# A ring of 20 batches in a kernel's second part, and a load moved between the value transfers of its first

## The reference

```python
x = x + xattn(_layernorm(x), ctx_1024, Wq, Wk, Wv, Wo)
x = x + ffn(_layernorm(x), weight, bias)

def ffn(x, weight, bias):
    w_scale = jnp.mean(jnp.abs(weight))
    q_weight = jnp.sign(weight) * (jnp.abs(weight) > 0.5 * w_scale)
    i_scale = jnp.max(jnp.abs(x)) / 127.0
    q_input = jnp.clip(jnp.round(x / i_scale), -128.0, 127.0)
    return jnp.einsum('bsk,ok->bso', q_input, q_weight) * w_scale * i_scale + bias
```

## Time and profile before

| | us |
|---|---|
| median of 3 runs | 1137.72 |
| profiled execution | 1138.31 |
| its span, first to last instruction | 1136.5 |
| PE busy | 1075.1 (95%) |
| DVE busy | 1015.8 (89%) |
| ACT busy | 963.0 (85%) |
| POOL busy | 729.6 (64%) |
| DMA queue of SP, share of 16 engines | 68.2% |
| moved | 262.97 MB |

### The profile page before, as it was taken

How to read it: one execution, slowest core, us unless ns; L and a number is a source line. 1 busy time by engine, 2 the same in 40 slices (tenths; PEclk the granted TensorE clock), 3 DMA queues, 4 the chain that set the end, 5 groups by cost and what they waited for, 6 DMA issues and landing times.

```text
span 1136.5 us, 44893 instructions
## 1 busy us (share of the span) xinstructions
PE 1075.1 (95%) x14007; PEld 865.5 (76%) x14007; DVE 1015.8 (89%) x1836; ACT 963.0 (85%) x2147; POOL 729.6 (64%) x1547
## 2 busy tenths in 40 slices
PE   7998999999999999999999999999599999999991
PEld 6997988988989988998889998998455555555540
DVE  4653898999999999999999999999789999999981
ACT  4564888988989889988899989999599999999980
POOL 4675998999999999999999999999500000000000
PEclk9999999999999999999999999999599999999996
DMA  8765366666676666766667653432049999999996
GB/s 290 228 176 162 85 205 189 211 189 214 177 223 183 210 216 187 221 194 198 207 195 222 184 154 106 121 104 67 1 180 408 421 424 426 426 407 371 411 395 267
DMA packets 119897, 262.97 MB, mean 231 GB/s; under 512 B 65193, under 2 KB 76649, under 8 KB 99378
## 3 DMA queue, kind: packets, MB, share of 16 engines
q1 hardware_dynamic: 119810, 262.44, 68.2%
q10 hardware_dynamic: 48, 0.07, 0.0%
HBM read 139.79 MB, written 122.64 MB: 231 GB/s over the span
## 4 chain that ended last, share of the span: by engine, by line
POOL 34%; issue 24%; PE 12%; ACT 9%; DMA 8%; DVE 6%; SPq 3%; POOLq 1%; ACTq 1%; DVEq 0%
POOL qa_sb L559 6%; POOL pw_sb L589 6%; POOL qr_sb L599 5%; ACT x_sb L789 5%; PE y_ps L1113 5%; DMA out_y<-x_sb 5%; POOL pw_sb L605 4%; POOL os_sb L619 3%; POOL o_sb L610 3%; DVE x_sb L1052 3%; ACT x_sb L772 2%; DMA x_sb<-out_y 2%; POOL ve_sb L576 2%; SPq L378 2%; POOL rs_sb L583 2%
## 5 line engine op out<-in xcount | busy, mean ns | idle before, releaser
L1258 PEld LDWEIGHTS xT_ps<-wqs,xT_sb 128*128 128x128 f32 x2048 | 239.2, 192 | 48.3 <-ACT xT_sb L725 48.3
L1258 PE MATMUL xT_ps<-wqs,xT_sb 128*128 128x128 f32 x2048 | 263.6, 282 | 2.8 <-ACT xT_sb L725 2.8
L978 DVE SCALAR_TENSOR_TENSOR x_sb<-x_sb,mv_sb,y_ps 128x512 f32 (+1 forms) x256 | 177.9, 736 | 3.2 <-PE y_ps L1250 3.2
L789 ACT ACTIVATE x_sb<-x_sb,mean 128x512 f32 (+1 forms) x256 | 168.7, 707 | 0.0
L1273 PE MATMUL pT_ps<-v_blk,pT_sb 128*128 128x102 f32 (+1 forms) x1280 | 163.6, 275 | 0.0
L689 ACT ACTIVATE sq_sb<-x_sb 128x512 bf16 (+1 forms) x256 | 160.8, 628 | 1.0 <-DVE x_sb L978 0.8
L1273 PEld LDWEIGHTS pT_ps<-v_blk,pT_sb 128*128 128x128 f32 x1280 | 155.2, 194 | 1.7 <-ACT pT_sb L738 1.0
L985 DVE TENSOR_REDUCE amax<-x_sb (+1 forms) x128 | 155.1, 1213 | 0.0
L748 ACT ACTIVATE e_sb<-e_sb,rs_sb 128x308 f32<-128x308 f32 x256 | 127.3, 544 | 16.2 <-DVE e_sb L961 6.6
L725 ACT ACTIVATE xT_sb<-xT_ps 128x1024 f32<-128x1024 f32 x128 | 131.3, 1026 | 3.0 <-PE xT_ps L1180 2.9
L1317 PE MATMUL sc_ps<-wT,x_sb 64*128 64x512 f16 x1024 | 133.5, 380 | 0.1
(11 more groups left out here) (140 smaller groups left out, 2286.0 us busy)
## 6 DMA issues: line engine op xcount, KB each, us to landing
out_y<-x_sb SPq DMA_DIRECT2D x112, 1024.0 KB, 10.2
x_sb<-in_x SPq DMA_DIRECT2D x128, 512.0 KB, 5.1
x_sb<-out_y SPq DMA_DIRECT2D x48, 1024.0 KB, 15.3
x_sb<-in_ctx SPq DMA_DIRECT2D x38, 256.0 KB, 4.5
k_blk<-k_scr SPq DMA_DIRECT2D x256, 9.6 KB, 1.7
v_blk<-v_scr SPq DMA_DIRECT2D x256, 10.2 KB
v_scr<-x_sb SPq DMA_DIRECT2D x38, 68.0 KB, 3.1
k_scr<-x_sb SPq DMA_DIRECT2D x38, 64.0 KB, 3.4
```

Source lines behind the costliest of these rows:

```text
L789: act.activation(u_sb[:, k % 2, t, :], x1_sb[:, bass.ds(x1_turn(g, k) + t * E, E)], ACT.Identity, bias=stat_of(mean1, j, t, back)).then_in ...
L978: dve.scalar_tensor_tensor(out=x1_at(kj, gj, t), in0=x_sb[:, kj // 2, 2 * (kj % 2) + t, :], scalar=mv_sb[:, kj, t, 0:1], in1=y_ps[:, t, :] ...
L1258: last = pe.matmul(bank[0][:, t * HD:(t + 1) * HD], xT_sb[:, t, c, :], wqs[:, c, :], start=c == 0, stop=c == EC - 1)
```

## The change

The ring x1_sb gets 20 slots, of which the last four are x_sb: x1_sb grows by four batches and x_sb becomes its tail, so the sum is the same. The temporaries of the second part move to the place of the first part's working tiles (from xT_sb on; four tables are moved so that the allocation covers them). In the first part x1_sb still turns over its first 16 slots (KEPT_TURNS = 4). In the second part, RING is 5, and four of the stored batches are read into x's slots as soon as `added_t` says that x is no longer needed there; the other 44 are read twenty batches behind a slot's result, not sixteen.

In the first part the first half of the next batch's x is issued between the eighth and the ninth of the twelve value pieces. A cycle of SP was: both halves of x(b), store, 12 values of b-1, 4 keys of b. It becomes: second half of x(b), store, 8 values of b-1, first half of x(b+1), 4 values of b-1, 4 keys of b.

```diff
-SLOTS = 16
-KEPT = SLOTS
+KEPT = 16
+KEPT_TURNS = KEPT // XS
+SLOTS = KEPT + XS
 RING = SLOTS // XS
...
-        x_sb = sb("x_sb", [P, XS, TPB, E])
...
         x1_sb = sb("x1_sb", [P, SLOTS * TPB * E])
+        x_sb = x1_sb[:, KEPT * TPB * E:].rearrange("p (k t e) -> p k t e", k=XS, t=TPB)
+
+        with nc.sbuf_tensor("qm_sb", [P, 2, 2, E], F32) as qm_sb, \
+                nc.sbuf_tensor("q16T_sb", [P, 2 * TPB, EC, P], F16) as q16T_sb, \
+                nc.sbuf_tensor("u_sb", [P, 2, TPB, E], F32) as u_sb, \
+                nc.sbuf_tensor("st_a", [P, NT], F32) as st_sb:
+            pass
...
         def x1_turn(g, k):

-            return ((g + (B - KEPT) // XS) % RING) * (XS * TPB * E) + k * TPB * E
+            return (g % RING) * (XS * TPB * E) + k * TPB * E
...
+            def x_half(b, k, n):
+
+                at_least(sp, added_t, 4 * (b - XS) + 2 * n + 2)
+                sp.dma_start(x_sb[:, k, 2 * n:2 * n + 2, :].rearrange("p t e -> p (t e)"),
+                             xv[bass.ds(b, 1), :, 2 * n:2 * n + 2, :].rearrange("b p t e -> p (b t e)"))\
+                  .then_inc(x_in[2 * k + n], 16)
+
             def batch_step(b, k, g, store=True):

-                for n in range(2):
-                    at_least(sp, added_t, 4 * (b - XS) + 2 * n + 2)
-                    sp.dma_start(x_sb[:, k, 2 * n:2 * n + 2, :].rearrange("p t e -> p (t e)"),
-                                 xv[bass.ds(b, 1), :, 2 * n:2 * n + 2, :].rearrange("b p t e -> p (b t e)"))\
-                      .then_inc(x_in[2 * k + n], 16)
+                x_half(b, k, 1)
                 if store:
                     store_x1(b - XS, k, g - 1)
+                v_fetch(b - 1, k - 1, SEGS[:8])
+                if not isinstance(b, int) or b + 1 < B:
+                    x_half(b + 1, (k + 1) % XS, 0)
+                v_step(b - 1, k - 1, SEGS[8:])
+                k_fetch(b, k)
...
+            x_half(XS, 0, 0)
             with sp.Fori(1, (B - KEPT) // XS + 1) as g:
                 for k in range(XS):
                     batch_step(g * XS + k, k, g)
-                    v_fetch(g * XS + k - 1, k - 1)
-                    k_fetch(g * XS + k, k)
...
+            for k in range(XS):
+                sp.wait_ge(added_t, 4 * (B - XS + k) + 4)
+                sp.dma_start(x1_sb[:, (KEPT + k) * TPB * E:(KEPT + k + 1) * TPB * E],
+                             ov[k].rearrange("p t e -> p (t e)")).then_inc(x1_in[k], 16)
```

More of the change, by code:

```diff
@@ L150, in build @@
         v_blk = sb("v_blk", [P, 2, CHUNKS, max(HEADS_OF), VC])
+        qcos = sb("qcos", [P, TPB, D])
+        qsin = sb("qsin", [P, TPB, D])
+        wqs = sb("wqs", [P, EC, HD])
+        wst = sb("wst", [P, 2, E], F32R)
         bn_sb = sb("bn_sb", [P, 2, 2, 6])
@@ L384, in k_fetch, with v_fetch @@
                 k_step(b, k)
[L386 removed]
+            def v_fetch(b, k, segs=SEGS):
                 at_least(sp, pv_done, 2 * (b - 2) + 2)
[L389 removed]
+                v_step(b, k, segs)
             sp.wait_ge(zeroed, ZEROED)
@@ L492, in two_back @@
                     x1_back(j + (n + m) // XS, (n + m) % XS)
-            for j in range(0, SLOTS, 2):
+            for k in range(XS):
+                sp.wait_ge(added_t, 4 * (B - XS + k) + 4)
+                sp.dma_start(x1_sb[:, (KEPT + k) * TPB * E:(KEPT + k + 1) * TPB * E],
+                             ov[k].rearrange("p t e -> p (t e)")).then_inc(x1_in[k], 16)
+            for j in range(0, KEPT, 2):
                 two_out(j // XS, j % XS, True)
@@ L498, in _ @@
                     two_back(n // XS, n % XS)
-            with sp.Fori(RING, (B - SLOTS) // XS) as g:
+            FULL = (B - SLOTS + 2) // XS
+            with sp.Fori(KEPT_TURNS, FULL) as g:
                 for k in range(0, XS, 2):
@@ L502, in _ @@
                     two_back(g + (k - 2) // XS + RING, (k - 2) % XS)
-            for j in range(B - SLOTS, B, 2):
+            for j in range(FULL * XS, B, 2):
                 two_out(j // XS, j % XS, False)
@@ L795, in turn @@
                 left = B - j if isinstance(j, int) else B
-                mean_back = not isinstance(j, int) or j + 1 >= SLOTS
+                mean_back = not isinstance(j, int) or j + 1 >= KEPT
                 if left > 2:
@@ L809, in _ @@
             add_mean(0, 0, range(TPB), False)
-            for j in range(SLOTS):
-                turn(j // XS, j % XS, j + 2 >= SLOTS)
-            with act.Fori(RING, B // XS - 1) as g:
+            for j in range(KEPT):
+                turn(j // XS, j % XS, j + 2 >= KEPT)
+            with act.Fori(KEPT_TURNS, B // XS - 1) as g:
                 for k in range(XS):
@@ L1081, in _ @@
             quantise(0, 1, False)
-            for j in range(SLOTS):
-                turn(j // XS, j % XS, j + 2 >= SLOTS)
-            with dve.Fori(RING, B // XS - 1) as g:
+            for j in range(KEPT):
+                turn(j // XS, j % XS, j + 2 >= KEPT)
+            with dve.Fori(KEPT_TURNS, B // XS - 1) as g:
                 for k in range(XS):
```

34 lines of the change are left out of this document (13 added, 21 removed).

## The result

The changed kernel takes 1147.05 us, the median of seven runs (1145.3 to 1150.6); the kernel before, run beside it, 1136.8 us (1132.96 to 1142.96). The ratio is 1.0088, interval 1.0063 to 1.0114: slower by about 0.9%. The profiled execution took 1145.95 us, its span is 1144.2 us (before 1138.31 and 1136.5). Of the experiments' executions one, of store_after_values_2, took 2093.38 us where its other four took 1113.96 to 1120.84; it is left out of the ratio.

A forecast was written before the change was run, and what follows sets the result against it. SP's issuing was taken to pace the first part and a queue of results to end the second. From 1138.3 us, -10 (first part) and -10 (ring) gave 1118.3, forecast as 1118.5 us; range 1114 to 1131.

The forecast's parts named there:

- What bounds the first part: First part, 130 to 660 us: SP's issuing sets the pace, 5.508 us a step against 5.397 without stores; whole loss 10.5 us.
- The ring: Second part: four reads go out early beside idle queues and leave the full queue, saving 9.8 to 11.0 us, taken as 10.
- The queue still ends last: End of second part: of 22.2 us of queue after the last add, 12 remain, so results still end the kernel.
- The new modulus: Second part, ACT: a few more register instructions of 74 ns stay covered; 0.19 us per batch of delay would be free.
- The early reads: Between the parts: four reads into x's old space, 4.2 MB, expected between 785 and 820 us, costing nothing.
- full queue later than 20 us after its begin: Second part: a sign that would show the prediction wrong, as would a rate below 400 GB/s.
- The reordered half gets earlier, and the values are late next: First part: x's half comes 4.1 us earlier; values' slack falls from 3.1 to 1.3 to 2.5 us, so PE waits for them.
- the point from which it decides: SP between store and next load: added cost outweighs the gains from 0.26 us per batch on, a cycle of 11.27 us.
- by bytes, 0.5 MB less is 0.5 / 0.42 = 1.2 us less stall per batch: SP's cycle, values behind the store: taken at half, -0.6 us a batch, enough for PE to set the pace; gain 10 us.
- the 2.67 us: SP's cycle: extra time of twelve value pieces behind a store, 2 MB queued, over those behind one half alone, read as stall.
- the stall grows: Rival, chance 0.15: SP meets a full queue twice, x's half between the pieces; 0.24 to 0.65 us a batch, worked case 1147.
- The stall stays: Rival, chance 0.25: the stall belongs to the store, not bytes; SP's cycle stays 11.0 us, first part gains 2, total 1126.

The follow-up runs named there:

- store_after_values: Kernel before with the ring of 20 and the store moved behind the twelve values, ahead of the keys: 1118.09 us, ratio 0.9855; repeated (suffix _2), 1117.02 us, ratio 0.9841.
- ring_only: Kernel before with only the ring of 20 added, its first part issuing in the old order: 1127.17 us, ratio 0.9932.
- order_only: Kernel before with only the reordered loads, keeping the ring of 16 and the old place of the temporaries: 1155.23 us, ratio 1.0196.
- half_after_values: Changed kernel with the next batch's first half of x issued behind all twelve values, ahead of the keys: 1144.78 us, ratio 1.0084.
- long_pieces_last: Kernel before with the ring of 20 and the value pieces of 76 and 51 rows issued last: 1126.17 us in one execution.
- half_between_store_last: Changed kernel with its store moved behind the twelve values: 1116.29 us, ratio 0.9832; repeated (suffix _2), 1115.08 us, ratio 0.983.
- both_ahead_next_half: Changed kernel with the next batch's first half of x moved ahead of the store, behind this batch's second half: 1169.44 us in one execution.
- store_first: Kernel before with the ring of 20 and the store issued ahead of both halves of x: 1196.17 us in one execution.
- half_behind_store: Changed kernel with the next batch's first half of x right behind the store, ahead of all twelve values: 1151.75 us in one execution.
- store_halves: Kernel before with the ring of 20 and the store issued as two transfers of 0.5 MB: 1154.44 us in one execution.

## Why the prediction was wrong

**What bounds the first part: right.** SP's issuing. The changed kernel and ring_only differ in nothing but SP's order, and by 20 us; a store in another place, or one issue fewer for SP, brings the steps to the 5.40 us that the earlier trace rows gave as the floor.

**The ring: right.** Four reads off a full queue were to give 10 us, between 9.8 and 11.0 by the earlier trace rows; the second part is 11.5 us shorter (ring_only: 11.1 in the profile, 8.7 in time; counted from order_only, which has no ring, 7.9 in the profile and 12 in time by the ratios 1.0196 and 1.0088). The reason for a price near the best stretch does not hold, though: reads and results are mixed in the fast stretch too (8 of each issued from 940 to 980 us, at 426 GB/s; 8 results and 6 reads from 1020 to 1060, at 381). The queue still ends last, with 1143.68 - 1130.14 = 13.5 us behind the last add, where some 12 were forecast. The new modulus cost nothing to be seen. The early reads went out from 814.23 us and the last of them at about 835.6, later than the 785 to 820 us forecast by the 20 us that the first part had lost; the last of them landed at 840.5, before the first result was issued at 852.03, so they were free all the same. The sign "full queue later than 20 us after its begin" was badly set: the stretch from the start of the second part to a full queue is 25 us in the kernel before (823 to 848) and 25 us in the changed one (843 to 868).

**The reordered half gets earlier, and the values are late next: right.** PE's waits for x are gone, its waits for v are there. That this slack would be used up once, after which SP's cycle sets the pace, was right too, and the point from which it decides, 0.26 us a batch, was well placed: at +0.50 us in the cycle (0.42 by the steps) the kernel is slower.

**The step that failed** is the one that sized SP's cycle: "by bytes, 0.5 MB less is 0.5 / 0.42 = 1.2 us less stall per batch", taken at half, -0.6 us. It came out at +0.50 us. The mechanism behind the term was wrong, not only its size. I had read the earlier trace rows as a stall in proportion to the bytes queued ahead. There is a hold that begins about 1 us after a store's issue and ends at a nearly fixed time after it, 4.2 us with two halves ahead, 3.8 with one. The 0.5 MB less did end it earlier, by 0.44 us. But only two pieces got through meanwhile instead of four, so two more, at about 0.47 us each with their gaps, remained to be issued afterwards: 2 x 0.47 - 0.44 = +0.5 us. That is how the time adds up; why fewer get through stays open.

The kernel before had shown enough to doubt the term. First, the 2.67 us were not all stall. The pieces of the earlier trace rows are issued behind the loop, where batch numbers are constants, and are quicker to issue: twelve take 4.26 us there and 5.17 us undisturbed in the loop (store_after_values). So 6.93 - 5.17 = 1.8 us of that row were stall, 1.4 in the mean. Second, the batch just before has no store but both halves, 1 MB, right ahead of its pieces, and they are as quick as behind one half:

```profile
659.06 0.83 SPq L443 DMA_DIRECT2D x_sb<-in_x  x2
659.94 4.25 SPq L378 DMA_DIRECT2D v_blk<-v_scr  x12
```

Third, I never asked for the pieces one by one. They would have shown an unheld first piece, four slow ones and seven quick ones, which a stall in proportion to the bytes ahead does not explain; and in the loop's first batch, the only place with one half in front of a store, the two long issues of the changed kernel:

```profile
132.38 0.33 SPq L378 DMA_DIRECT2D v_blk<-v_scr  x1
132.90 1.50 SPq L378 DMA_DIRECT2D v_blk<-v_scr  x1
134.60 1.16 SPq L378 DMA_DIRECT2D v_blk<-v_scr  x1
135.95 0.30 SPq L378 DMA_DIRECT2D v_blk<-v_scr  x1
```

That batch had shown +0.24 to +0.65 us. It was set aside as a single sample, for an estimate that had no sample at all.

**The rival that came true** is "the stall grows", given 0.15, with the price of 0.24 to 0.65 us a batch from that row; its worked case was 1147 us, and the kernel takes 1147.05. Its story was only half right: it put the cost down to SP meeting a full queue twice, with x's half between the pieces. half_after_values has no half between them and loses nearly as much; the four pieces behind the half are quick (1.57 us). The price was right because it came from a row, which did not depend on the story; that the worked case meets the time so closely is luck, since its bounds of 0.24 and 0.65 us spanned some 20 us.

**"The stall stays"** rested on the store in front as the cause and not the bytes. In this it was nearer to the truth than the forecast, though its cycle of 11.0 us was not. Few queues behind the piece of 51 rows have no part in it: in long_pieces_last that piece takes about 0.25 us once it is last, and others are held in its place. By the Trainium skill ("DMA: Bandwidth & Descriptors", section "Why a DMA increments its semaphore by 16 and not by 1") such a piece would sit on 3 engines; no row here shows on how many it does.

The second part moved 410 GB/s, where the kernel before had 412. The bound of about 358 GB/s for such transfers in the Trainium skill (same page, section "Where 436 GB/s comes from") does not agree with either.

**The range** of 1114 to 1131 left this rival out. With the only row of the kind on its side, the chance of 0.15 was too low, and a step with bounds of either sign around a threshold should have kept the range open to both.

## What to carry to other kernels

Where an engine's queue of issues sets the pace, read the issues one by one: a merged group hides which of them is held, and where a hold ends at a nearly fixed time, what has not been issued by then is added behind it, so removing bytes in front need not help. Put a store behind the small transfers that someone is waiting for, and look at what the store's own wait would hold up; here the changed kernel with its store moved so (half_between_store_last) went from +10 us to -19. A single row that shows the very arrangement you are about to make outweighs an argument from proportion.

## What the runs showed of the hardware

A 1 MB store from SBUF to HBM holds the transfers issued after it, for a while, at their issue. Those that start within 0.8 us of the store's issue take their usual 0.25 to 0.4 us. From about 1 us on (0.86 at the earliest) issues are slow: two of them, 1209 and 1255 ns in the mean of the changed kernel, or, where two halves of x stand right ahead of the store (before, ring_only, long_pieces_last, both_ahead_next_half), two to four of 0.4 to 1.0 us in the mean and up to 2.0 singly. The hold ends 2.7 to 3.1 us after the store's issue where no load stands right ahead of it (store_first, store_after_values, half_between_store_last_2), about 3.8 us after it with 0.5 MB right ahead (4.1 in half_behind_store) and 4.0 to 4.3 us with 1 MB. It met value pieces, key pieces and a half of x alike, comes with the store in two halves, and reaches SP's queue when ACT's queue issues the store. It is not there behind 1 MB of loads. Five of these kernels (long_pieces_last, store_halves, store_first, half_behind_store, both_ahead_next_half) ran once each; their holds are means over some 40 cycles of one trace.

Why it is so stays open: nothing here shows what the issuing queue waits for, or why the hold takes fewer and longer issues with one half in front than with two.
